# A two-layer recurrent block on one core: token maxima by one GpSimd instruction, and retention results kept as heads by tokens

## What is computed

```python
def _L1_attn_ref(x, W_qk, b_qk, W_v, b_v, W_g, b_g, W_o, b_o):    # 16 heads, keys of 8, values of 16
    ...
    scores = jnp.einsum('bhtd,bhsd->bhts', q, k) * mask
    denom = jnp.clip(jnp.abs(scores).sum(-1, keepdims=True), 1.0, 50000.0)
    scores = scores / denom
    ret = jnp.einsum('bhts,bhsv->bthv', scores, v)
    ret = ret * jax.lax.rsqrt(jnp.mean(ret * ret, axis=-1, keepdims=True) + EPS)
    y = ret.reshape(Bx, Tx, H * VD)
    gated = (x @ W_g + b_g) * y
    return gated @ W_o + b_o

def _L1_ffn_ref(...):                                             # 8 experts of 64 slots
    ...
    logits = jnp.einsum('bnd,esd->bnes', xn, sn)
    dispatch = jax.nn.softmax(logits, axis=1)                     # over the tokens
    combine = jax.nn.softmax(logits.reshape(b, n, e * s), axis=-1)  # over the 512 slots
    ...
    out = jnp.einsum('bmd,bnm->bnd', eo, combine)
```

## Time and profile before

| | |
|---|---|
| median of 3 runs | 1098.42 us (1098.21 to 1098.63) |
| the profiled execution | 1098.24 us |
| its span, first to last instruction | 1096.4 us |
| granted clock of TensorE, mean | 0.992 of full speed |
| instructions | 27975 |

### The profile page before, as it was taken

How to read it: one execution, slowest core, us unless ns; L and a number is a source line. 1 busy time by engine, 2 the same in 40 slices (tenths; PEclk the granted TensorE clock), 3 DMA queues, 4 the chain that set the end, 5 groups by cost and what they waited for, 6 DMA issues and landing times.

```text
span 1096.4 us, 27975 instructions
## 1 busy us (share of the span) xinstructions
PE 1062.8 (97%) x10436; PEld 832.9 (76%) x10436; DVE 960.2 (88%) x2074; ACT 773.0 (71%) x1450; POOL 606.9 (55%) x619
## 2 busy tenths in 40 slices
PE   5799999999999999999999999999999999999997
PEld 3478687787868778687787868778687787868776
DVE  3788989899898988989899898988989899898985
ACT  3476786767777676786767777676786767777674
POOL 2465547556474665547556474655647556474553
PEclk9899999999999999999999999999999999999998
DMA  6000000000000000000000000000000000000000
GB/s 257 11 2 11 1 20 3 1 21 1 21 1 11 11 1 22 1 12 10 2 21 1 21 1 2 20 2 21 2 11 11 2 20 2 21 1 2 11 1 20
DMA packets 18468, 16.97 MB, mean 15 GB/s; under 512 B 800, under 2 KB 17440, under 8 KB 18080
## 3 DMA queue, kind: packets, MB, share of 16 engines
q1 hardware_dynamic: 18336, 15.18, 4.2%
HBM read 10.98 MB, written 4.19 MB: 14 GB/s over the span
## 4 chain that ended last, share of the span: by engine, by line
PE 90%; DVE 6%; issue 1%; ACT 1%; POOL 0%; POOLq 0%; DVEq 0%; ACTq 0%
PE bank L1008 12%; PE bank L959 11%; PE bank L969 10%; PE bank_s L990 7%; PE bank L950 5%; PE bank L979 5%; PE bank L920 5%; PE bank L913 5%; PE bank L1035 3%; DVE ret L661 3%; PE bank L908 3%; PE bank L823 3%; PE bank L874 3%; PE bank L1018 3%; PE bank_s L993 2%; PE bank L854 2%
## 5 line engine op out<-in xcount | busy, mean ns | idle before, releaser
L329 POOL TENSOR_TENSOR ret_abs<-ret_abs 128x512 f32<-128x512 f32 x128 | 168.7, 1318 | 238.2 <-ACT ret_abs L485 238.2
L661 DVE TENSOR_TENSOR ret<-bank_s,k_sb 128x1536 f32<-128x1536 f32 x128 | 223.9, 1749 | 23.7 <-PE bank L1008 14.8
L334 POOL TENSOR_TENSOR urs<-uvar,mhalf 128x16 f32<-128x16 f32 x64 | 185.3, 2903 | 91.8 <-DVE uvar L677 91.8
L485 ACT ACTIVATE ret_abs<-ret 128x1536 f32<-128x1536 f32 x128 | 189.6, 1481 | 8.8 <-DVE ret L661 8.8
L959 PE MATMUL bank<-slotsT,w_sb 128*128 128x128 f32 x1024 | 140.9, 281 | 0.3 <-DVE hact L726 0.3
L969 PEld LDWEIGHTS bank<-w_sb,hact 128*128 128x128 f32 x1024 | 125.5, 192 | 14.7 <-issue 13.9
L969 PE MATMUL bank<-w_sb,hact 128*128 128x128 f32 x1024 | 134.1, 277 | 0.0
L959 PEld LDWEIGHTS bank<-slotsT,w_sb 128*128 128x128 f32 x1024 | 124.3, 192 | 10.3 <-issue 7.4
L340 POOL TENSOR_SCALAR dT<-dT,drec 128x256 f32<-128x256 f32 x128 | 83.4, 665 | 48.6 <-DVE drec L721 48.4
L1008 PE MATMUL bank<-ret,vrow 128*32 128x256 f32 (+1 forms) x2048 | 108.6, 329 | 0.3 <-DVE hact L726 0.2
L990 PE MATMUL bank_s<-qT,km 32*128 32x256 f32 x1024 | 91.4, 426 | 5.0 <-DVE ret L661 5.0
(11 more groups left out here) (143 smaller groups left out, 2397.9 us busy)
## 6 DMA issues: line engine op xcount, KB each, us to landing
x_sb<-x SPq DMA_DIRECT2D x16, 256.0 KB, 2.8
w_sb<-w SPq DMA_DIRECT2D x2, 2048.0 KB, 14.8
out<-attn SPq DMA_DIRECT2D x16, 256.0 KB, 2.3
v_sb<-vectors SPq DMA_DIRECT2D x1, 832.0 KB, 8.1
w_sb<-weights SPq DMA_DIRECT2D x1, 512.0 KB, 5.3
k_sb<-consts SPq DMA_DIRECT2D x1, 466.0 KB, 6.6
w_sb<-weights SPq DMA_DIRECT2D x1, 320.0 KB, 3.2
slot_sb<-slot_rows SPq DMA_DIRECT2D x1, 256.0 KB, 3.5
```

The costliest lines, as they stand in the source:

```text
L329: pool.tensor_tensor(both[:, :, P:SEQ], both[:, :, P:SEQ], both[:, :, SEQ:3 * P], ALU.add)\
L334: pool.tensor_tensor(urs[:, j], uvar[:, j], mhalf[:], ALU.pow).then_inc(ready["urs"].sem, 1)
L485: act.activation(ret_abs[:, q % MR], ret[:, q % MR], ACT.Abs).then_inc(ready["ab"].sem, 1)
L661: dve.tensor_tensor(ret[:, q % MR], bank_s[:, :, 0:3 * P], causal.unsqueeze(1).broadcast_to([P, Q, 3 * P]), ALU.mult)\
```

## The change

Slot maxima: mxT, rmax, rB and ScalarE's rBc go. One GpSimd instruction, `partition_all_reduce` with max, reads mx (128 x 512) and writes rB with each token's maximum in all partitions; `cs` subtracts it.

Retention: two neighbouring quads (a duo) now accumulate in one bank, `g` writing results in columns 0 to 255 and sums of absolute values, repeated over a head's 16 rows, in 256 to 511. The results stay heads by tokens. ScalarE squares them (usq), one matmul with a constant block matrix "heads" (1/16 within a head's rows) gives mean squares in each of the head's rows (ms), VectorE clips the denominators (den), multiplies by the gate (ug) and adds the mean squares and the squared scaled denominators (rx; the square on ScalarE, dsq). Per pair ScalarE then takes ln and exp of -0.5 times it, each at 128 x 1024 (ln, rs), and VectorE multiplies (gated), two instructions. RTc, row, rowd, urs, gatedT and gTc go. The gate is made as channels by tokens (gT, gTb) and vg makes the values alone.

ORDER and BANK are written anew; the diff shows GpSimd's rows of ORDER alone.

```diff
+    "POOL": [("rstd2", 0, 1), ("rnorm", 0, 1), ("rstd", 0, 0), ("km", 0, 1), ("km", 1, 1), ("km", 2, 1),
+             ("dn", 0, 1), ("km", 3, 1), ("add", 0, 1), ("mixa", 0, 0), ("add", 1, 1), ("dn", 1, 1), ("dn", 2, 1),
+             ("dn", 3, 1), ("km", 4, 1), ("km", 5, 1), ("add", 2, 1), ("add", 3, 1), ("rBc", 0, 1), ("km", 6, 1),
+             ("km", 7, 1), ("add", 4, 1), ("add", 5, 1), ("add", 6, 1), ("add", 7, 1)],
...
-            def urs_(p, par, j):
-                pool.wait_ge(*ready["uvar"](p, j))
-                pool.tensor_tensor(urs[:, j], uvar[:, j], mhalf[:], ALU.pow).then_inc(ready["urs"].sem, 1)
+            def rBc(p, par, k):
+                pool.wait_ge(*ready["mx"](p, 2))
+                since(pool, ready["cs"], p - 1, 3)
+                pool.partition_all_reduce(rB[:], mx[:], P, bass.bass_isa.ReduceOp.max).then_inc(ready["rBc"].sem, 1)
 
...
-            def RTc(p, par, g):
...
-            def usq_(p, par, j):
...
-            def gTc(p, par, b):
...
+            def gTb(p, par, u):
+                bank = bank_of("gT", p, u)
+                since(act, ready["ug"], p - 1, 2 + u)
+                act.activation(grow[:, u], bank[:], ACT.Identity, bias=V["b_g"][:, u:u + 1]).then_inc(ready["gTb"].sem, 1)
+
+            def usq_(p, par, h):
+                act.wait_ge(*filled["g"](p, 2 * h + 1))
+                since(act, filled["ms"], *((p, h - 2) if h >= 2 else (p - 1, h + 2)))
+                act.activation(usq[:, h % 2], banks[BANK["g", 2 * h]][:, 0:SEQ], ACT.Square).then_inc(ready["usq"].sem, 1)
+
+            def dsq(p, par, h):
+                act.wait_ge(*ready["den"](p, h))
+                act.activation(den[:, h % 2], den[:, h % 2], ACT.Square, scale=RET_EPS ** 0.5).then_inc(ready["dsq"].sem, 1)
+
+            def ln(p, par, k):
+                act.wait_ge(*ready["rx"](p, DUOS - 1))
+                act.activation(rx[:], rx[:], ACT.Ln).then_inc(ready["ln"].sem, 1)
+
+            def rs(p, par, k):
+
+                act.wait_ge(*ready["ln"](p))
+                act.activation(rx[:], rx[:], ACT.Exp, scale=-0.5).then_inc(ready["rs"].sem, 1)
 
...
+            def vgc(p, par, b):
+                bank = bank_of("vg", p, b)
+                since(dve, filled["g"], p - 1, 4 * b + 3)
+                dve.tensor_tensor(vrow[:, 2 * b:2 * b + 2, :, 0:VD], bank[:].rearrange("p (i h v) -> p i h v", i=2, h=HEADS),
+                                  V["b_v"].rearrange("p (h v) -> p h v", h=HEADS).unsqueeze(1).broadcast_to([P, 2, HEADS, VD]),
+                                  ALU.add).then_inc(ready["vgc"].sem, 1)
 
...
-            def rowd(p, par, j):
...
+            def den_(p, par, h):
+                dve.wait_ge(*ready["usq"](p, h))
+                since(dve, ready["rx"], *((p, h - 2) if h >= 2 else (p - 1, h + 2)))
+                dve.tensor_scalar(den[:, h % 2], banks[BANK["g", 2 * h]][:, SEQ:], 1.0, 50000.0, ALU.max, ALU.min)\
+                   .then_inc(ready["den"].sem, 1)
+
+            def ug_(p, par, h):
+                b, u = divmod(h, 2)
+                dve.wait_ge(*ready["usq"](p, h))
+                dve.wait_ge(*ready["gTb"](p, u))
+                since(dve, filled["o"], p - 1, b)
+                dve.tensor_tensor(ug[:, h], banks[BANK["g", 2 * h]][:, 0:SEQ], grow[:, u, b * SEQ:(b + 1) * SEQ], ALU.mult)\
+                   .then_inc(ready["ug"].sem, 1)
+
+            def rx_(p, par, h):
+                dve.wait_ge(*filled["ms"](p, h))
+                dve.wait_ge(*ready["dsq"](p, h))
+                dve.wait_ge(*ready["ug"](p, h))
+                since(dve, ready["gated"], p - 1, h // 2)
+                dve.tensor_tensor(rx[:, h], banks[BANK["g", 2 * h]][:, SEQ:], den[:, h % 2], ALU.add).then_inc(ready["rx"].sem, 1)
+
+            def gated_(p, par, b):
+                dve.wait_ge(*ready["rs"](p))
+                duos = slice(2 * b, 2 * b + 2)
+                dve.tensor_tensor(ug[:, duos], ug[:, duos], rx[:, duos], ALU.mult).then_inc(ready["gated"].sem, 1)
 
...
             def mx_(p, par, i):
                 dve.wait_ge(*ready["LTc"](p, i + 1))
                 if i == 0:
-                    since(dve, filled["mxT"], p - 1)
+                    since(dve, ready["rBc"], p - 1)
                 else:
...
-            def rmax_(p, par, k):
...
                 dve.wait_ge(*ready["rBc"](p))
                 dve.wait_ge(*ready["DTe"](p, m))
                 dve.wait_ge(*ready["mx"](p, 2))
-                dve.tensor_tensor(cT[:, m], cT[:, m], rB[:], ALU.add).then_inc(ready["cs"].sem, 1)
+                dve.tensor_tensor(cT[:, m], cT[:, m], rB[:], ALU.subtract).then_inc(ready["cs"].sem, 1)
 
...
+            def vg(p, par, b):
                 pe.wait_ge(*ready["xn2Tc"](p))
-                bank = claim("vg", p, j)
-                pe.matmul(bank[:], xn2T[:, j // 2, (j % 2) * P:(j % 2 + 1) * P], W["vg"], start=True, stop=True)\
-                  .then_inc(filled["vg"].sem, 1)
+                bank = claim("vg", p, b)
+                for i in range(2):
+                    ins = pe.matmul(bank[:, i * SEQ:(i + 1) * SEQ], xn2T[:, b, i * P:(i + 1) * P], W["vg"][:, 0:HEADS * VD],
+                                    start=True, stop=True)
+                ins.then_inc(filled["vg"].sem, 1)
+
+            def gT(p, par, u):
+                pe.wait_ge(*ready["xn2Tc"](p))
+                bank = claim("gT", p, u)
+                pe.matmul(bank[:], W["vg"][:, HEADS * VD + u * P:HEADS * VD + (u + 1) * P], xn2T[:], start=True, stop=True)\
+                  .then_inc(filled["gT"].sem, 1)
 
...
-            def mxT(p, par, k):
...
-            def rB_(p, par, k):
...
             def g(p, par, q):
-                b = q // Q
+                b, i = q // Q, q % 2
                 pe.wait_ge(*ready["add"](p, q))
-                pe.wait_ge(*ready["vgc"](p, 2 * b + 1))
-                bank = claim("g", p, q)
+                pe.wait_ge(*ready["vgc"](p, b))
+                bank = banks[BANK["g", q - 1]] if i else claim("g", p, q)
+
+
+                spread = vrow[:].rearrange("p j h v -> p j (h v)")
                 for phase in range(3):
                     for n in range(Q):
                         src = (ret, ret_abs)[phase // 2]
                         sblock = phase % 2
-                        left = vrow[:, 2 * b + sblock, Q * (q % Q) + n] if phase < 2 else K["count"]
+                        at = (Q * (q % Q) + n) * HT - i * VD
+                        left = spread[:, 2 * b + sblock, at:at + HT] if phase < 2 else K["count"][:, (1 - i) * VD:(1 - i) * VD + HT]
                         cols = (0, SEQ) if sblock == 0 else (SEQ, 3 * P)
-                        ins = pe.matmul(bank[n * HT:(n + 1) * HT, sblock * P:SEQ], left,
-                                        src[:, q % MR, n, cols[0]:cols[1]], start=(phase == 0), stop=(phase == 2))
+                        into = (phase // 2 * SEQ + sblock * P, (phase // 2 + 1) * SEQ)
+                        ins = pe.matmul(bank[n * HT:(n + 1) * HT, into[0]:into[1]], left, src[:, q % MR, n, cols[0]:cols[1]],
+                                        start=(i == 0 and phase == 0), stop=(i == 1 and phase == 2))
                 ins.then_inc(filled["g"].sem, 1)
 
...
-            def row(p, par, j):
...
-            def gatedT_(p, par, b):
...
+            def ms(p, par, h):
+                pe.wait_ge(*ready["den"](p, h))
+                pe.wait_ge(*ready["ug"](p, h))
+                pe.matmul(banks[BANK["g", 2 * h]][:, SEQ:], K["heads"], usq[:, h % 2], start=True, stop=True)\
+                  .then_inc(filled["ms"].sem, 1)
 
             def o(p, par, b):
-                pe.wait_ge(*ready["gTc"](p, b))
+                pe.wait_ge(*ready["gated"](p, b))
                 bank = claim("o", p, b)
                 for i in range(2):
                     for v in range(2):
-                        ins = pe.matmul(bank[:, i * C:(i + 1) * C], gatedT[:, b, i, v], W["o"][:, v * C:(v + 1) * C],
...
-    put("count", (np.arange(HT) == VD)[None, :].repeat(P, 0))
+
+    put("count", (np.arange(3 * VD) // VD == 1)[None, :].repeat(P, 0))
+    put("heads", (np.arange(P)[:, None] // VD == np.arange(P)[None, :] // VD) / VD)
```

171 lines of the change are left out of this document (45 added, 126 removed), and 46 rows, old and new, of tables (BANK, ORDER).

## The result

The changed kernel takes **1182.2 us** (median of 4, 1180.7 to 1184.8) against 1098.3 for the kernel before: ratio 1.0766, 95% interval 1.0746 to 1.0787. It is 84 us slower, and 114 us above my forecast. All times here are medians of fast runs; the one run counted as slow, in after_two_moves, is left out.

What follows compares the result with a forecast made beforehand. TensorE was taken to bound the kernel: 1098.24 us less 30.9 of its work and 2.5 at the end gives 1064.8, plus 3 for the new order, 1068 us. The range ran from 1062 to 1158.

Steps and rivals of the forecast that it cites:

- What bounds the kernel: Whole kernel: TensorE, busy 97%, sets the time; a saving on another engine brings nothing by itself.
- TensorE's work: Per pair of sequences: 3.66 us of transposes go, 1.73 of block-matrix matmuls come; 1.93 us saved, 30.9 over 16.
- start and tail: Before the first pair and after the last g: nothing lost at the start, 2.5 us saved at the end.
- GpSimd's hold: GpSimd between add 3 and km 6: two code switches and the maximum, together 10.2 us, range 1.1 to 24.
- A small transfer's landing, near 2.8 us: Each of GpSimd's two code switches around the maximum: 2.8 us, between nothing and 8.1.
- The middle, 4.6: GpSimd's all-partition maximum: 4.6 us, the middle between bounds of 1.14 and 8.0.
- Its cover, 10.8 us, and 16 us for each us above it: TensorE's queued work up to g 4 hides 10.8 us of GpSimd's switches and maximum; each us beyond costs 16.
- costed at nothing: VectorE had 12% spare and gets more; ScalarE's about +3 us per pair fits its 20 us idle: no cost.
- 3 us for the new order: Allowance for waits in the new instruction order: 0.2 us per pair on top of the old 0.3.
- rival B: ScalarE's three table loads in a row make out 0 or LT late: 25 us, giving 1093; chance 0.06.
- A: Switches and maximum hold GpSimd beyond 10.8 us, so TensorE waits every pair: 1158 us; chance 0.39 beyond breakeven.
- C: TensorE idles the saved time at ret and quad: up to 1.9 us per pair, 1098 us; chance 0.04.

Runs made afterwards that it cites:

- after_two_moves: The changed kernel, real maximum kept, with the two moves on VectorE of b0_order: 1148.9 us, runs from 1140.6 to 1152.0.
- b0_short_adds: The plain copy with GpSimd's eight adds of the absolute halves cut from 512 columns to 16, leaving out that part of the sums: 1067.9 us.
- max_on_tensor_2: Changed kernel, but maxima by TensorE's transposes as in the kernel before, placed in other banks, with VectorE's order of b0_order; full computation: 1106.0 us.
- b0_order: The plain copy with VectorE's attention output ahead of the mixes and the gate and spin products moved away from GpSimd's adds 6 and 7: 1086.75 us.
- b14_busy: The changed kernel with a copy for the maximum and six unread powers around it, holding GpSimd 14.5 us without a code switch: 1172.9 us.
- plain copy: The changed kernel with GpSimd's all-partition maximum replaced by one elementwise copy, without code switches: 1113.1 us.

## Why the prediction was wrong, point by point

**What bounds the kernel** (TensorE; nothing else gains): right. Every gain and loss in the runs is TensorE's work, its waits or its clock.

**TensorE's work**, -1.93 us per pair, with start and tail: the total came right, in part by luck. b0_short_adds, which has all of the new TensorE work, came to 1067.9 against 1068. But the 1068 hold 0.5 us of waits per pair, 8 us, and that run has none. Its step is 64.29 us; the step of before is 65.94 with 0.28 of waits, so TensorE saves 1.37 us per pair and not 1.93, 22 us instead of 30.9. The difference is in places of the order: both vg groups take 1.03 and 1.05 us in the chain where I priced 0.86, an LT group 1.06 for 0.86, an ms 0.63 for 0.43. The old waits and a better end make up for it. max_on_tensor_2 with its two groups of transposes is 19.2 us above b0_order, 1.20 per pair where the rows give 0.44 + 0.58 = 1.02.

**GpSimd's hold**: this step failed in two terms. "A small transfer's landing, near 2.8 us" for a switch: measured 6.0 and 7.0. "The middle, 4.6" for the maximum: measured 1.80, nearer to the lower bound. Together 14.8 us instead of 10.2. The lower bound rested on a mix of 1139 ns; the same mix takes 694 in the changed kernel, and a copy of 128x512 in the maximum's place 624. The range of the hold, 1.1 to 24, contained it; the choice inside it was made from an argument (code is small beside tables) that no row bore out. The Trainium skill, page "GPSIMD Engine Reference", 2.1 Instruction dispatch, names about 6 us, and I kept it as a rival. The traces have 6.0 and 7.0.

**Its cover, 10.8 us, and 16 us for each us above it**: near, by two errors that cancel. The hold less TensorE's two stops is 14.57 - 2.85 in the pair above and 14.46 - 2.73 in b14_busy: 11.7 us in both, so the cover was 0.9 us longer than I counted. From the end of score 0 TensorE takes about 17.8 us to quad 6 instead of 17.4, and add 3 is through after about 4.8 instead of 5.1. Below that length the hold is not free either: at 10.6 us it cost 13.4 by a collision. And the rule had no term for the clock. The stops bring the lower clock with them, 1.6 us on g 4 and g 5 in that pair. (2.85 - 0.25 for a wait that the plain copy has there too + 1.6) x 16 = 67, against 64 by the rule with 14.8 us and 69 measured.

**VectorE and ScalarE "costed at nothing", and 3 us for the new order**: this failed by more than the hold's price. The new order costs 45 us, 39 of them waits: 2.46 us per pair where I allowed 0.2 on top of 0.3. I looked at VectorE's share, 88%, with less work to come, and took that as cover. What I did not do is lay GpSimd's adds beside VectorE's two-input instructions in the new order. Rows of before, which I didn't put beside each other, show what it costs:

```profile
L556 DVE SCALAR_TENSOR_TENSOR mix<-xnT,v_sb,mix 128x512 f32<-128x512 f32 x32 | 40.9, 1316 | 21.2 <-POOL mix L297 21.2
L705 DVE TENSOR_TENSOR mx<-mx,cT 128x512 f32<-128x512 f32 x32 | 37.3, 1167 | 1.7
L606 DVE SCALAR_TENSOR_TENSOR prob<-prob 128x512 f32<-128x512 f32 x16 | 16.3, 1022 | 0.0
L612 DVE SCALAR_TENSOR_TENSOR spin<-spin,prob 128x512 f32<-128x512 f32 x16 | 10.8, 676 | 0.3 <-ACT spin L413 0.3
```

spin (the spin product) is a form like mix and takes half of its time, so collisions were in it already. In the new order mx fell from 1167 to 691 ns, but the gate product rose from 1022 to 1567 and the spin product from 676 to 1223. These two end in x1 and xn2, a chain on which TensorE waits. ScalarE's part held: 6 table loads of 1283 ns per pair, and rival B fell: b0_short_adds has the same loads in the same places, and its TensorE waits for none of them.

**Rivals.** A was the mechanism of 69 of the 114 us. My end for it, 1158, fell short by 24 since it stood on the sum without the order's waits, and it is that near only because the hold in it was 1.8 us too long, 16.6 us: with the measured 14.8 us it gives 1068 + 64 - 3 = 1129. No rival held the second mechanism, and the two add. C (TensorE idles elsewhere in the new order) had the right idea, with the wrong place (ret and quad, 0.25 us) and the wrong size: up to 1.9 per pair allowed, 2.46 found.
